# A routed two-block network on one core: routing steps given per group, and the dense experts' weights applied before the product instead of after it

## The reference, cut to what matters

```python
x = x + L0_conv(ln_c(x))          # mixing along rows and columns
t = t + L0_ffn(ln_t(t))           # 8 experts, top 2, and a shared one
x = x + L1_conv(ln_c(x))          # attention in each image: softmax(k q^T) v, times gamma
t = t + L1_ffn(ln_t(t))           # switch layer: 16 experts, top 1

# L1_ffn on xf = ln_t(t), N = 4608, E = 16
probs = softmax(xf @ switch_w.T + switch_b)
route_probs, routes = max(probs), argmax(probs)
pos = position of the token among those of its expert, in token order
keep = pos < int(1.2 * N / E)                      # 345
y = expert_w[routes] @ xf + expert_b[routes]
out = where(keep, y, xf) * route_probs
```

## Time and profile before

| | us |
|---|---|
| median of 3 runs | 482.83 |
| lowest and highest of them | 482.43, 485.3 |
| the profiled execution | 481.0 |
| its span | 479.0 |
| mean granted clock of TensorE | 0.849 of full |

### The profile page before, as it was taken

One profiled execution on the slowest core, in us unless ns is written; L12 is line 12 of the kernel. 1 busy time (PEld: TensorE's weight loads), 2 busy tenths in 40 slices (PEclk: granted clock), 3 DMA queues, 4 the chain that ended last, 5 costly groups with the idle time before them and its releaser, 6 DMA issues.

```text
span 479.0 us, 6876 instructions
## 1 busy us (share of the span) xinstructions
PE 376.5 (79%) x2123; PEld 318.9 (67%) x2123; DVE 315.8 (66%) x1009; ACT 162.4 (34%) x345; POOL 122.6 (26%) x139
## 2 busy tenths in 40 slices
PE   0875494986999999998657999998989516986961
PEld 0775493984888888887346999997889416832420
DVE  6874786777565556569566577775666632569886
ACT  2452124435223332332215455673644402300000
POOL 2333026101800000003000761101054770057710
PEclk9999755556899999999955799999998556999886
DMA  6980000000910000000021101011000118713223
GB/s 169 263 284 1 16 8 1 1 0 8 410 44 1 0 0 0 0 0 0 3 49 25 26 19 35 19 35 27 2 31 21 44 50 263 267 37 99 55 61 99
DMA packets 22905, 29.64 MB, mean 62 GB/s; under 512 B 4120, under 2 KB 18265, under 8 KB 22622
## 3 DMA queue, kind: packets, MB, share of 16 engines
q1 hardware_dynamic: 18846, 22.62, 15.5%
q0 software_dynamic: 1728, 3.54, 2.5%
q10 hardware_dynamic: 2304, 3.15, 1.8%
HBM read 13.48 MB, written 12.78 MB: 55 GB/s over the span
## 4 chain that ended last, share of the span: by engine, by line
PE 25%; DVE 15%; POOL 3%; issue 3%; ACT 3%; DMA 2%; SPq 0%; DVEq 0%; ACTq 0%
DVE R L1308 7%; PE ps L1510 7%; POOL slots L1033 3%; PE ps L1478 3%; PE ps L1623 2%; PE ps L1591 2%; PE ps L1490 2%; DVE R L1297 1%; PE ps L1497 1%; DVE mx L1110 1%; PE ps L1603 1%; DVE K L1125 1%; PE ps L1460 1%; PE ps L1459 1%; PE ps L1458 1%
## 5 line engine op out<-in xcount | busy, mean ns | idle before, releaser
L155 POOL TENSOR_TENSOR rstd<-sm,neg_half 128x9 f32<-128x9 f32 (+1 forms) x20 | 32.4, 1620 | 223.8 <-DVE sm L149 223.7
L749 PE MATMUL ps<-wide,gu_w 128*128 (+1 forms) x108 | 52.2, 483 | 2.5 <-PEq L646 2.5
L1510 PE MATMUL ps<-V,wide 128*128 128x129 f32 x400 | 53.2, 283 | 0.0
L821 ACT ACTIVATE s<-ps 128x384 f32<-128x384 f32 (+1 forms) x60 | 29.5, 491 | 68.2 <-PE ps L753 67.8
L780 PE MATMUL ps<-h,wd 128*128 128x384 f32 x120 | 50.2, 500 | 1.6 <-DVE h L865 1.2
L1510 PEld LDWEIGHTS ps<-V,wide 128*128 128x128 f32 x400 | 50.1, 198 | 0.0
L860 DVE TENSOR_TENSOR t<-ps,s 128x384 f32<-128x384 f32 x48 | 26.7, 557 | 30.7 <-ACT s L821 30.5
L1308 DVE SCALAR_TENSOR_TENSOR R<-ps,dense_w,R 128x128 f32<-128x128 f32 x144 | 37.7, 342 | 7.7 <-PE ps L1623 7.7
L1110 DVE TENSOR_REDUCE mx<-ps 128x1 f32<-128x576 f32 (+1 forms) x40 | 29.9, 751 | 12.5 <-PE ps L1478 12.3
L753 PE MATMUL ps<-wide,gu_w 128*128 (+1 forms) x108 | 37.2, 344 | 0.3 <-DVE t L860 0.3
L750 PE MATMUL ps<-wide,gu_w 128*128 (+1 forms) x108 | 37.2, 345 | 0.0
(11 more groups left out here) (196 smaller groups left out, 840.4 us busy)
## 6 DMA issues: line engine op xcount, KB each, us to landing
slots<-zrow SPq DMA_DIRECT2D x7, 768.0 KB, 8.9
xe<-slots SPq DMA_DIRECT2D x16, 192.0 KB, 5.1
slots<-wide ACTq DMA_DIRECT2D x16, 192.0 KB, 3.1
xall<-in_x SPq DMA_DIRECT2D x8, 288.0 KB, 3.5
out<-R SPq DMA_DIRECT2D x12, 192.0 KB, 2.4
Q<-sQK SPq DMA_DIRECT2D x8, 144.0 KB, 2.4
K<-sQK SPq DMA_DIRECT2D x8, 144.0 KB, 2.5
ew<-in_ew SPq DMA_DIRECT2D x1, 1024.0 KB
```

Of the source, the lines that this page charges most:

```text
L155: nc.gpsimd.tensor_tensor(rstd[p][:rows, :n], sm[p][:rows, 5, :n], neg_half[:rows, :n], ALU.pow).then_inc(rstd_ok, 1)
L749: nc.tensor.matmul(o, gu_w[0][:, w], xTH[:, at], start=True, stop=False)
L821: nc.scalar.activation(s4[q][:r], bank[q][:r, :CH], ACT.Silu).then_inc(s_ok[q], 1)
L1510: last = nc.tensor.matmul(bank[6 + k // 3][:, k % 3 * (C + 1):(k % 3 + 1) * (C + 1)], PT[n % 2][:, jk, i0:i0 + P], V[n % 2][:, jk, :], sta ...
```

## The change

It has three parts.

**Routing steps per group.** A table gives each group its step: `ROUTER_AT = (5, 6, 8, 10)` and `PLACE_AT = (6, 7, 9, 11)`, where before they were 5, 7, 9, 11 and 6, 8, 10, 12. The loop has one step less. The moments follow the ninth `bn_stats` at once (`k == 2`) instead of at the step's end. ScalarE's normalizing becomes `apply6(g, c)`: the first third in part 4 of the step of the statistics, the second at that step's end, the last at the start of the router's step. GpSimd's order changes, and with it where a third transposes' bank is used.

```diff
+        ROUTER_AT, PLACE_AT = (5, 6, 8, 10), (6, 7, 9, 11)
...
-            return bank[0] if c == 2 and 2 * g + 5 > B else bank[4 + c % 2]
+            return bank[0] if c == 2 and 2 * g + 4 >= B else bank[4 + c % 2]
...
+                nc.gpsimd.memset(wR[:].bitcast(F32), 0.0).then_inc(wz9, 1)
                 rstd6(0)
                 rstd6(1)
-                scatter(0, range(GT))
+                scatter(0, range(SPLIT))
                 rstd6(2)
-                scatter(1, range(0, SPLIT))
+                scatter(0, range(SPLIT, GT))
+                scatter(1, range(GT))
                 rstd6(3)
-                scatter(1, range(SPLIT, GT))
                 scatter(2, range(GT))
...
+                def apply6(g, c):
+                    if c == 0:
+                        act.wait_ge(rs6, 2 * g + 2)
+                        if g == NG - 1:
+                            act.wait_ge(pv, NB_SS * (B - 1))
+                        elif g >= 2:
+                            act.wait_ge(sc6[g % 2], 16 * GT * (g // 2))
...
+                        if k == 0 and at_step(n, ROUTER_AT) is not None:
+                            apply6(at_step(n, ROUTER_AT), 2)
...
+                        if k == 4 and behind(n, 3) is not None:
+                            apply6(behind(n, 3), 0)
...
+                    if behind(n, 3) is not None:
+                        apply6(behind(n, 3), 1)
...
-                    g = behind(n, 5)
+                    g = at_step(n, ROUTER_AT)
...
+                        if k == 4 and at_step(n, PLACE_AT) is not None:
+                            counts(at_step(n, PLACE_AT))
                         if k == (4 if n < B else 1) and g is not None:
                             router_transposes(g, 2)
-                        if k == 4 and behind(n, 6) is not None:
-                            counts(behind(n, 6))
```

```diff
+                pe.wait_ge(dw9, 2)
+                for t in range(GT):
+                    o = psum[3][:E1, t * P:(t + 1) * P] if t < 8 else bank[0][:E1, :P]
+                    last = nc.tensor.transpose(o, dense_w[:, t, :], ident)
+                last.then_inc(wt9, 1)
                 for e in range(E1):
...
+                    elif e == 0:
+                        pe.wait_ge(wc9, 1)
```

```diff
+        masked = xeT + [spare[:, e * CH:(e + 1) * CH] for e in range(NYE)]
+        spread_banks = [bank[j] for j in (0, 1, 2, 3, 6, 7)]
...
+                def mask(c, e):
+                    i = E1 * c + e
+                    dve.wait_ge(bc9, i + 1)
+                    if i >= NMASK:
+                        dve.wait_ge(mp9, i - NMASK + 1)
+                    nc.vector.tensor_tensor(masked[i % NMASK], spread_banks[i % NBC][:, :CH], xT3[c][:], ALU.mult).then_inc(mk9, 1)
...
+                for j in range(NYE):
+                    dve.wait_ge(st7[j], 16 * len(range(j, E1, NYE)))
+                for c in range(3):
+                    for e in range(E1):
+                        mask(c, e)
+                        if (c, e) == (0, 1):
+                            add_dropped()
+                        if c and e == 2:
+                            add_dense(c - 1)
+                        if c and e % 5 == 4:
+                            combine(3 * (c - 1) + e // 5)
...
+                    nc.tensor.matmul(spread_banks[i % NBC][:, :CH], selc[:, e:e + 1].to_broadcast([P, P]),
+                                     wR[:, c * CH:(c + 1) * CH], start=True, stop=True).then_inc(bc9, 1)
...
+                for i in range(NBC - 1):
+                    spread(i)
+                for i in range(3 * E1):
...
+                        spread(i + NBC - 1)
...
+                    pe.wait_ge(mk9, i + 1)
+                    for t in range(3):
+                        last = nc.tensor.matmul(bank[NBANK + c % 2][:, t * P:(t + 1) * P], masked[i % NMASK][:, t * P:(t + 1) * P],
+                                                ew[:, e, :], start=e == 0 and t == 0, stop=False, skip_group_check=True)
```

More of the change, by code:

```diff
@@ L993, in behind, with at_step @@
             return g if (n - lag) % 2 == 0 and 0 <= g < NG else None
+        def at_step(n, steps):
+            return steps.index(n) if n in steps else None
         def xn_buffer(g):
@@ L1323, in _ @@
                     at = slice(GT * ROUTED + 3 * c, GT * ROUTED + 3 * c + 3)
                     nc.vector.tensor_tensor(R[:, at, :], R[:, at, :],
-                                            bank[6 + c % 2][:, :CH].rearrange("p (t c) -> p t c", c=C),
+                                            bank[NBANK + c % 2][:, :CH].rearrange("p (t c) -> p t c", c=C),
                                             ALU.add).then_inc(d8o, 1)
-                    for part in range(3 * c, 3 * c + 3):
-                        combine(part)
+                for j in range(NYE):
+                    dve.wait_ge(st7[j], 16 * len(range(j, E1, NYE)))
@@ new lines, in _ @@
+                for c in range(3):
[7 more added lines that the diff above has]
+                            combine(3 * (c - 1) + e // 5)
+                add_dense(2)
+                for part in range(6, 9):
+                    combine(part)
@@ L1343, in router_copy @@
                     nc.scalar.activation(router_in(g, c)[:], l_bank(g, c)[:, :CH], ACT.Copy).then_inc(l_xt, 1)
+                def apply6(g, c):
+                    if c == 0:
+                        act.wait_ge(rs6, 2 * g + 2)
[3 more added lines that the diff above has]
+                            act.wait_ge(sc6[g % 2], 16 * GT * (g // 2))
+                        else:
+                            act.wait_ge(t_ps, 3 * (g + 3))
+                    for t in range(3 * c, 3 * c + 3):
+                        ins = nc.scalar.activation(xn_buffer(g)[:, t, :], R[:, GT * g + t, :], ACT.Identity,
+                                                   bias=nmr[g % 2][:, t:t + 1], scale=rstd[g % 2][:, t:t + 1])
+                    ins.then_inc(xn6, 1)
                 for n in range(-3, LAST):
-                    g = behind(n, 4)
                     for k in range(NB_SS):
@@ L1520, in router_transposes @@
                         banks_empty()
-                    elif c == 2 and 2 * g + 5 > B + 2:
+                    elif c == 2 and 2 * g + 2 >= B:
                         pe.wait_ge(lg_ok, 3 * g)
@@ new lines, in _ @@
+                for i in range(3 * E1):
+                    c, e = divmod(i, E1)
+                    if i + NBC - 1 < 3 * E1:
+                        spread(i + NBC - 1)
+                    if i == 2 * E1:
+                        pe.wait_ge(d8o, 1)
+                    pe.wait_ge(mk9, i + 1)
+                    for t in range(3):
+                        last = nc.tensor.matmul(bank[NBANK + c % 2][:, t * P:(t + 1) * P], masked[i % NMASK][:, t * P:(t + 1) * P],
+                                                ew[:, e, :], start=e == 0 and t == 0, stop=False, skip_group_check=True)
+                    last.then_inc(mp9, 1)
+                    if e == E1 - 1:
+                        for t in range(3):
+                            last = nc.tensor.matmul(bank[NBANK + c % 2][:, t * P:(t + 1) * P],
+                                                    wT[:, (3 * c + t) * P:(3 * c + t + 1) * P], ebr[:],
+                                                    start=False, stop=True, skip_group_check=True)
+                        last.then_inc(b9, 1)
```

136 lines of the change are left out of this document (55 added, 81 removed).

## The result

Over four runs each on one chip the changed kernel takes 491.31 us (median, 490.22 to 492.85), the kernel before 482.63 us (481.8 to 485.3). The ratio is 1.0175, with a 95% interval of 1.0131 to 1.0218: slower, by 1.3 to 2.2%. A second measurement (experiment 5) gave 491.59 against 482.93 us, ratio 1.0180 (1.0113 to 1.0247). The profiled execution took 492.85 us for a span of 490.4 us, where before it was 481.0 for 479.0.

What follows compares the result with a forecast made beforehand. The end was bound by four links: GpSimd's scatter queue, the expert loop, the last stores' landing, and the dense part on VectorE. 481.0 + 11.9 (later landing) - 3.9 (dense part) = 489.0 as profiled, stated as 490; range 479 to 497.

Steps and rivals of the forecast that it cites:

- Rival A: TensorE's wait for group 0's scatters is short; loop starts at 402.8, landing 3.6 us later, 480.7 us; chance 0.18.
- Rival B: Change pays: routing earlier, dense part at VectorE's pace, a unit under 0.7 us on TensorE; 467 us; chance 0.10.
- rival C: Waits between units break TensorE's pipeline (1.0 us a unit), or the clock falls for 8 us; 497 us; chance 0.10.
- Step 6, +2.8 us: Routing step 6: transposes, logit products and a wait take 2.8 us, moving the maxima row from 346.5 to 349.3.
- First scatter 353.9, last of group 0 at 368.3, TensorE held until 371.8: Routing: group 0's later scatters hold `xn[0]`, so TensorE, there at about 364.5, stands at router 2's transposes until 371.8.
- TensorE through 10.9 us after the wait: Routing, after the wait until 371.8: at a lowered clock TensorE finishes transposes, `attend` and logit products at 382.7.
- image 7 added 2.0 us later: Routing: VectorE has added image 7 at 384.7 instead of 370.7, after TensorE is through at 382.7.
- Five things before the loop, 5.7 us: Ahead of the expert loop: nine transposes, copies to `wR` and `wT`, subtraction; together 5.7 us, loop starting at 411.1.
- Loop 19.0 us less some 0.4: Expert loop: 19.0 us before, some 0.4 us saved at its start because all rows lie ready.
- No mask before T, third mask at T + 4.1: T, when all expert-row stores have landed (434.4): masks start after it, dropped-token additions hold the third until T + 4.1.
- Dense part, a unit at 0.84 us: Masked dense part: each of 48 units costs TensorE 0.84 us, the bound changing from VectorE to TensorE.
- Clock 0.3 us: Dense part: 0.3 us allowed for TensorE's clock, in a sum ending 45.0 us after the stores' landing.

Runs made afterwards that it cites:

- experiment 5: The changed kernel run again as it is, as reference: 491.59 against 482.93 us on chip B (1.0180), 521.75 against 509.52 on chip C (1.0255).
- experiment 3: Changed kernel with group 2's normalized tokens put in tiles no scatter reads: 483.86 us on chip B (ratio 1.0022 to the kernel before), 1.0306 on chip A.
- experiment 1: Changed kernel with its routing part undone, masked dense part kept: 475.75 us on chip B (ratio 0.9875 to the kernel before), 516.98 on chip A (1.0166).
- experiment 4: Changed kernel with masks 0 to 3 ahead of the stores' landing: 1.0236 (chip A), 1.0206 (C); "both" adds the old routing: 475.30 us, 0.9863 (B).

## Why the prediction was right, and where its steps were off

The forecast was 490 us and slower; measured were 491.31. The mechanism on which it stood was the right one: TensorE stands idle at group 2's transposes, held by `xn[0]` and so by group 0's scatters, and experiment 3 shows that this hold makes half of the loss or more. That the median lies only 1.3 us from the forecast is in part luck. The forecast added 8.0 us to the profiled execution of before, and the two profiled spans differ by 11.4 us. The medians differ by 8.7 only because before was profiled 1.6 us below its median and the changed kernel 1.5 above.

Rival A was the forecast without that wait, which is the kernel of experiment 3. It gave `dense_w` at 397.1, landing 3.6 us later and 480.7 us; measured were 397.9, 4.2 us and 480.8 in the profiled execution, but 483.9 as the median. The agreement is in part luck: it had image 7 at 371 and GpSimd's queue as the hold until 381.2. Image 7 came at 377.3, and the variance (382.23) and the end of group 1's scatters (382.25) met by chance. Rival B's premise (a unit under 0.7 us) fell: 0.845. Of rival C neither form came.

Step by step, predicted and measured:

- *Step 6, +2.8 us*: the maxima row goes from 346.51 to 350.77, +4.3, but 1.3 of that are there already in step 4 (317.73 against 316.46). Step 6 itself is +3.0. The small parts were taken at 0, with 1 as the end, and the 1.3 is not shown to be theirs: in three profiles with the old order (experiment 1 on A and on B, experiment 4 with both) ScalarE's copy of step 4 starts at 316.8, 317.9 and 318.6, so runs alone differ by as much.
- *First scatter 353.9, last of group 0 at 368.3, TensorE held until 371.8*: 355.34, 369.41, 373.03. The wait was put at 7.3 us and is 5.1. I had left out that `attend(6, 4)` also stands ahead of the transposes, so thirty instructions and not twenty. It cost the forecast nothing: the end of the wait is set by the scatters, not by when TensorE arrives.
- *TensorE through 10.9 us after the wait* (the terms stated add up to 10.7), *image 7 added 2.0 us later*: to the end of the last `attend` it is 12.0 us. The two `attend` at 380.61 were put at 1.5 and 1.1 us and took 4.4, since the clock stayed down for them; I had let it come back before them. The terms ahead of them took 0.5 us less than stated. Then the six last logit instructions (1.30 us), which the sum doesn't name, stood ahead of VectorE's last additions, which were over 1.0 us behind them. Together 14.4 us for 12.9, and with a wait that ended 1.2 us late image 7 is added at 387.4 instead of 384.7. Most of this distance stays: variance 392.0 for 389.5, `dense_w` 407.7 for 405.4.
- *Five things before the loop, 5.7 us*: from `dense_w` to the loop's start 6.4 us, since the nine transposes ran at the low clock (2.08 us for the 1.6 taken). The subtraction, bounded at 0.56 and 1.7 and taken at 1.4, took 1.41. The loop starts at 414.05 for 411.1.
- *Loop 19.0 us less some 0.4*: 18.4. Behind it the landing came 1.0 us sooner than before, which I had not in the sum and which hides a part of the error: 436.2 for 434.4, 13.7 us late for 11.9.
- *No mask before T, third mask at T + 4.1*: the first mask started at 435.51, 0.7 us ahead of the first gather that I took for T, and the third unit's product at T + 3.2. So this term was 0.9 us too long.
- *Dense part, a unit at 0.84 us*: 0.845. *Clock 0.3 us*: this term was mis-sized most. Three units behind the first two (439.41 to 444.38) took 1.65 us each instead of 0.845, 2.4 us for the 0.3; TensorE ended 46.7 us after the landing for 45.0. Elsewhere the same code from landing to end takes 51.8 us, 0.8 less than my 52.6: in experiment 1 on chip B with the clock at 1.00 in the first units, in experiments 3 and 5 on chip B with it at about half there (0.50, and 0.58 and 0.56), but on the first two units only, which end by the time the third mask is there. So here a low clock cost something only where TensorE was waited for. The tail of 7.5 us is exact.

The larger errors have one kind of cause, how long TensorE stays at its lower clock after a wait and what it does meanwhile. They made the kernel slower than the sum, 492.4 us instead of 489.0 for an execution like the profiled one, with the late scatters (1.2 us) beside them and some 3 us of smaller errors the other way.

The Trainium skill, in "TensorE: Matmul & The Clock Gate", section "Step-by-step: what each phase is for", has matmuls stay in program order. The trace agrees with it: the `attend` behind the transposes started at 376.04 only, after they had gone, though the last of its inputs, ScalarE's exponentials, had been ready at 362.6 and TensorE stood idle from 367.9 to 373.0.

## What to carry to other kernels

Before an operation is moved ahead in an in-order queue, look up what its input waits for and the whole chain behind that; here a router moved one step forward waited for nine scatters that the change itself had made later. A buffer shared by two groups is such a chain, and a spare tile that is idle at that time takes it away (7.7 us here, on chip B). And read two parts of one change apart: on chip B the kernel with the old routing was 1.2% faster than the kernel before (0.5 to 2.0%), and the new schedule made it 3% slower than that. On chip A the same kernel was 1.7% slower than the kernel before, so this gain does not hold on every chip.

## What the runs showed of the hardware

What I had not expected is the 26 us between chips, for the same kernel. On the slower ones the traces show stretches in which instructions start singly, about 0.7 us or a multiple of it apart. TensorE in the changed kernel on chip C, then a window of the same stretch (columns as in rows 6):

```profile
460.66 0.37 PE L1677 MATMUL ps<-ew,wide 128*128 128x128 f32 x1 [1.03 <-issue]
462.80 0.37 PE L1677 MATMUL ps<-ew,wide 128*128 128x128 f32 x1 [1.76 <-issue]
...
467.01 0.48 PE L1661 MATMUL ps<-wR,selc 128*128 128x384 f32 x1 [2.42 <-issue]
```
```profile
464.00:472.00 8.00, 1.59 (x4) 0.94 (x4) 0.00 (x0) 0.00 (x0) 6.12 (x7) 0.50 0.21 53
```

Four matmul instructions in 8 us, where the same kernel has 68 later (488 to 496), at a granted clock of 0.50, while GpSimd issues its seven gathers as always. With the old dense part, on chip D, it is VectorE's instructions that start singly, while TensorE waits for them for 20.7 us; GpSimd beside it keeps its 1.25 us from one gather to the next:

```profile
466.67 0.35 DVE L1325 SCALAR_TENSOR_TENSOR R<-ps,dense_w,R 128x128 f32<-128x128 f32 x1 [1.03 <-DVE R L1325]
467.38 0.35 DVE L1325 SCALAR_TENSOR_TENSOR R<-ps,dense_w,R 128x128 f32<-128x128 f32 x1 [0.36 <-DVE R L1325]
468.77 0.35 DVE L1325 SCALAR_TENSOR_TENSOR R<-ps,dense_w,R 128x128 f32<-128x128 f32 x1 [1.04 <-issue]
...
462.70 0.94 POOL L1070 DMA_INDIRECT wide<-slots,gidx  x1 [0.30 <-issue]
```

The stretch lasts some 26 us with the masked dense part and some 20 with the old one. From the landing to the end it takes 79.9 to 81.3 us with the masked part on chips A and C (75.4 and 76.6 with early masks) and 73.8 to 77.3 with the old one on A, C and D, where it is 51.8 on chip B and 56.5 in the trace of before. So on such chips the masked part loses its gain. Pauses lie in steps 7 to 12 too: in the kernel of experiment 1 the stores land 10.6 us later on chip A than on B. Why these chips do so, and whether the kernel before is stopped in the same place, stays open: it has no trace there, only its time.
